# The second attention stage and the FP4 stage of a fused kernel in one block, with FP4's first steps and weight transposes inside attention's last steps

## Chip, cores, metric

One core of a Trainium2 chip. The metric is the device time of one execution in microseconds; the matrix engine is TensorE (PE), the others are VectorE (DVE), ScalarE (ACT), GpSimd (POOL) and SyncE (SP), which issues the transfers. All engines run their own instruction lists in order and meet at semaphores.

## What is computed

Two layers on `x` of 4 x 1024 rows with 256 columns. Each layer is cross attention to a context of 77 rows with 16 heads of 16, then a feed-forward part, each with a layer norm before it and a residual after it:

```
x = x + xattn0(layernorm(x), ctx)          # softmax(q k^T / 4) v, then Wo
x = x + ffn_sine(layernorm(x))             # W1 256x1024, a sine term, relu, W2
x = x + xattn1(ctx, layernorm(x), mask)    # the same with a mask per row and key
x = x + ffn_fp4(layernorm(x))

def ffn_fp4(x):                            # blocks of 16 along the last dim
    gate = q4(x) @ q4(w_gate).T            # 256 -> 704
    y    = q4(x) @ q4(w_up).T
    return q4(silu(gate) * y) @ q4(w_down).T
# q4: scale = max|block| / 6, values rounded to 0, .5, 1, 1.5, 2, 3, 4, 6 times scale
```

## The kernel before

The rows of `x` stay in the core's memory as 32 tiles of 128 rows (`T` = 32). Four stages follow one another: `attention(l=0)`, `ffn_sine`, `attention(l=1)`, `ffn_fp4`. Each is a `nc.Block()` with one unrolled list of instructions for each engine, and at a block's end all engines meet. Each stage is a software pipeline written out by hand: `step(i)` on an engine does its part of several tiles.

**Attention.** In `step(i)` PE does: the scores of tile i (into banks `psS0` to `psS3`), the transposes of the normalised tile i+1 (`psQ`), `attended(i-2)` (transposes of `on`, the attention output, into `psY`), then for tile i-1 the transposes of the shifted scores in three groups through one bank `psT`, each group waiting until ACT's exp (`prob`) has emptied the bank, with the queries of tile i+1 behind the first group and `projected(i-2)` (times Wo, into `psY`) behind the second, and last softmax times V of tile i-1 (`psO`). DVE does `outputs(i-2)` (reciprocal of the sums and division of `psO`, giving `on`), the row maxima and the shift of tile i, the low part of `oTs` for tile i-2 (`attended_high` on ACT is its high part), statistics of tile i+3, the low part of the queries, the normalised tile i+2, and `residual(i-2)`. Steps 5 to 27 that are odd also quantise one of 12 pieces of the FP4 weights `w4` (`w4_scales`, `w4_powers` on DVE, `w4_scale_up`, `w4_rounding` on POOL; the first attention stage does the other 12). `step(32)` and `step(33)` drain the pipeline: in step 32 (i == T) the calls of `attended(30)` and, on ACT, `attended_high(30)` come after the three groups and the three exps.

**FP4.** At the start of its block PE transposes the quantised weights in 11 `groups` through five banks: eight of three 128 x 128 transposes for `wgu` (gate and up; ACT writes the high part, `weight_copy`, and DVE the low part, `weight_low`), three of four for `wdT` (down; no low part). 36 transposes in all. PE waits for all of these before its `step(i)`. The steps run from -10 to 34. DVE: `bn_stats` and `bn_aggr` of tile i+10, the block maxima of tile i+4 (`x_largest`, `x_scale`, `x_inverse`), `x_powers` of tile i+3, `x_low` of tile i+2, `hidden`, `h_largest` and the rest of quantising `hid` for tiles i and i-1, `residual(i-2)`. POOL: `deviations` for four tiles at once, `x_up` (i+4), `x_sum`, `x_rounded`, `x_down` (i+3, giving `xres`), `h_up`, `h_down`. ACT: `normalise` (i+5), `x_lowered` (i+3), `x_high` (i+2), `h_kick` (i), the silu (i+1), the copies of transposed `hid`. PE: the products of tile i with gate and up in three segments of 512, 512 and 384 columns (`psGU`), of six matmuls each, the transposes of `xres` of tile i+1 behind the first segment, the down products of tile i-3, the transposes of `hres` of tile i-2. SP stores four tiles at a time.

Each tile's `hid` needs the silu of its gate half; the silu of tile 1 stands behind `h_kick(0)` on ACT, which needs `h_exponents(0)` on DVE, `h_up(0)` on POOL and `h_inverse(0)` on DVE, so PE's products of tile 2 wait for the whole chain from `hid` of tile 0.

Of the kernel before, what the change touches and what calls it, by code (L numbers as in the profile page):

```python
# [5 lines left out]
P = 128  # L6
# [66 lines left out]
def build(nc, x_in, ctx_in, mask_in, att0_in, att1_in, w1_in, w2_in, w4_in, cols_in, rows_in,  # L73
          blockmask_in, headmask_in, ident_in, out):
    with ExitStack() as ctx:
# [3 lines left out]
        def sem(name):  # L79
# [20 lines left out]
        w_high, w_split, w4_max, w4_scale, w4_inv, w4_scaled, w4_val, w4_exp, w4_pow, w4_sum, w4_round = (  # L100
            sem(n) for n in ("w_high", "w_split", "w4_max", "w4_scale", "w4_inv", "w4_scaled", "w4_val", "w4_exp",
                             "w4_pow", "w4_sum", "w4_round"))
# [9 lines left out]
        with ExitStack() as early:  # L112

            own(early, "w1", [P, 2, KC, FF0], F32R)
            own(early, "w2", [P, 2, FF0 // P, D], F32R)
            with ExitStack() as keys:
                own(keys, "kblk0", [P, 2, B, KC, PAIR * KV], F32R)
                own(keys, "wo0", [P, 2, KC, D], F32R)
                attention(nc, sem, 0, g)
            ffn_sine(nc, sem, g)  # L120
        with ExitStack() as keys:
            own(keys, "kblk1", [P, 2, B, KC, PAIR * KV], F32R)
            own(keys, "wo1", [P, 2, KC, D], F32R)
            attention(nc, sem, 1, g)
        own(ctx, "wgu", [P, 2, KC, 2 * FF1], F32R)
        own(ctx, "wdT", [P, NF1, D])
        ffn_fp4(nc, sem, g)


class Context:  # L130


    def __init__(self, nc, sem, g, l, ctx, psK, psVT, psV):
        self.nc, self.g, self.l, self.psK, self.psVT, self.psV = nc, g, l, psK, psVT, psV
        self.k_mm, self.k_high, self.k_low, self.vT_mm, self.vT_ready, self.v_mm, self.vblk_done = (
            sem(f"b{l}_{n}") for n in ("k_mm", "k_high", "k_low", "vT_mm", "vT_ready", "v_mm", "vblk_done"))
        self.bias_mm, self.bias_done, self.wo_high, self.first_keys, self.more_keys = (
            sem(f"b{l}_{n}") for n in ("bias_mm", "bias_done", "wo_high", "first_keys", "more_keys"))
        self.kTs = ctx.enter_context(nc.sbuf_tensor(f"b{l}_kTs", [P, 2, KC, B * KV], F32R))
        self.vT = ctx.enter_context(nc.sbuf_tensor(f"b{l}_vT", [P, KC, B, 3 * KV], F32))  # L140
# [23 lines left out]
    def value_transposes(self, pe):  # L164

        pe.wait_ge(self.vT_ready, KC)
        for n, (c, h, _, _) in enumerate(V_SLOTS):
            if n == 1:
                pe.wait_ge(self.bias_done, 1)
# [8 lines left out]
    def key_copies(self, act):  # L178
        bk = C_BK + 2 * self.l
        for h in range(KC):  # L180
            act.wait_ge(self.k_mm, h + 1)
# [3 lines left out]
    def value_copies(self, act):  # L185
        for h in range(KC):
            act.wait_ge(self.vT_mm, h + 1)
# [4 lines left out]
    def projection_high(self, act):  # L192
        self.nc.scalar.copy(self.g[f"wo{self.l}"][:, 0], self.g["wat"][self.l][:, :, 2 * D:3 * D]).then_inc(self.wo_high, 1)

    def head_block(self, b, n):

        return (self.g[f"kblk{self.l}"][:, :, b, :, n * KV:(n + 1) * KV],
# [1338 lines left out]
```

## Time and profile before

| | |
|---|---|
| Median of 3 runs | 1014.23 us (1012.83 to 1015.88) |
| The profiled execution | 1008.32 us, span 1006.5 us |
| Busy, share of the span | PE 92%, DVE 83%, ACT 48%, POOL 46% |
| Mean granted clock of PE | 0.966 of full |
| First attention stage | ends at 257.5 us |
| Sine stage | to about 476 us |
| Second attention stage | ends at 732.6 us |
| FP4 stage | from there to the end |

The times of the trace are microseconds from the start of the span. The span is what the engines' instructions cover; 1.8 us lie around it. PE's busy time holds its pipeline's latency, so that a PE that is busy all the time need not be at its peak. "Granted clock" is the share of TensorE's full 2.4 GHz that it was given; a value between 0.5 and 1 in a stretch means that it changed within the stretch.

### The profile page before, as it was taken

How to read it: one execution, taken by the hardware profiler on the slowest of the kernel's cores; microseconds unless marked ns; L12 is line 12 of the kernel's file. 1: busy time of each engine (PE TensorE's matmuls, PEld its weight loads, DVE VectorE, ACT ScalarE, POOL GpSimd, SP SyncE). 2: the span in 40 equal slices, each digit the busy share in tenths (PEclk: the TensorE clock that was granted, in tenths of full speed). 3: DMA queues.
4: the chain of work that ended last, by engine and by line, in shares of the span. 5: the costliest groups of instructions: out<-in, count | busy, mean ns of one | idle time of the engine just before them, and what ended most of it. 6: DMA issues, size and time to landing. Idle time of an engine off the chain costs nothing. (4 is left out here: it accounts for less than half of the span.)

```text
span 1006.5 us, 20339 instructions
## 1 busy us (share of the span) xinstructions
PE 927.3 (92%) x7332; PEld 817.8 (81%) x7332; DVE 832.3 (83%) x2172; ACT 486.8 (48%) x1019; POOL 466.7 (46%) x663
## 2 busy tenths in 40 slices
PE   6899999998599999998899999999868999999997
PEld 4798998997488888887689898989756888888885
DVE  5899999995599999986789888988468889889874
ACT  2643443442288888886344343433244444444442
POOL 2233333330376666664223323333046777777662
PEclk9999999998699999999899999999869999999999
DMA  9020000000000000000100000000000000000000
GB/s 349 19 96 2 2 2 2 1 2 1 1 1 2 1 1 1 1 1 4 49 2 2 2 2 2 2 1 2 1 1 1 22 22 1 21 22 22 22 21 22
DMA packets 6083, 18.32 MB, mean 18 GB/s; under 512 B 864, under 2 KB 2784, under 8 KB 5472
## 3 DMA queue, kind: packets, MB, share of 16 engines
q1 hardware_dynamic: 5264, 16.52, 4.3%
q8 instruction: 59, 0.97, 0.4%
q10 hardware_dynamic: 720, 0.50, 0.2%
q14 instruction: 40, 0.33, 0.1%
HBM read 12.83 MB, written 4.19 MB: 17 GB/s over the span
## 5 line engine op out<-in xcount | busy, mean ns | idle before, releaser
L815 PE MATMUL a_psO<-vblk,a_prob 128*128 128x51 f32 (+1 forms) x1280 | 151.9, 275 | 0.0
L815 PEld LDWEIGHTS a_psO<-vblk,a_prob 128*128 128x128 f32 x1280 | 151.6, 196 | 0.0
L1408 PE MATMUL f_psGU<-wgu,f_xTs 128*128 128x512 f32 (+1 forms) x576 | 141.7, 391 | 3.9 <-ACT f_silu L1360 2.6
L504 DVE TENSOR_REDUCE a_mx<-a_psS 128x4 f32<-128x308 f32 x256 | 115.0, 470 | 18.1 <-PE a_psS L737 16.5
L676 ACT COPY a_xTs<-a_psQ 128x256 f32<-128x256 f32 x64 | 23.9, 373 | 205.5 <-PE a_psQ L746 205.5
L687 ACT ACTIVATE a_prob<-a_psT 128x512 f32<-128x512 f32 (+1 forms) x192 | 101.1, 526 | 44.1 <-PE a_psT L793 42.7
L1408 PEld LDWEIGHTS f_psGU<-wgu,f_xTs 128*128 128x128 f32 x576 | 104.0, 193 | 19.6 <-DVE f_xTs L1172 4.6
L793 PE MATMUL a_psT<-ident,a_shifted 128*128 128x128 f32 x640 | 106.8, 282 | 12.4 <-ACT a_prob L687 9.5
L512 DVE TENSOR_TENSOR a_shifted<-a_psS,a_mx 128x308 f32<-128x308 f32 x256 | 114.4, 467 | 0.0
L1034 PEld LDWEIGHTS s_psY<-w,s_hid 128*128 128x128 f32 x768 | 99.4, 188 | 16.6 <-POOL s_hid L952 12.3
L1034 PE MATMUL s_psY<-w,s_hid 128*128 128x256 f32 x768 | 104.0, 284 | 5.7 <-POOL s_hid L952 5.0
L1022 PE MATMUL s_psH<-s_xTs,w 128*128 128x512 f32 x384 | 101.8, 402 | 2.7 <-DVE s_xTs L933 2.0
L952 POOL TENSOR_TENSOR s_hid<-wat,s_hid 128x512 fp32r<-128x512 f32 x64 | 86.1, 1346 | 39.1 <-ACT wat L989 39.1
L793 PEld LDWEIGHTS a_psT<-ident,a_shifted 128*128 128x128 f32 x640 | 72.7, 142 | 27.3 <-ACT a_prob L687 27.3
L1425 PE MATMUL f_psY<-wdT,f_hTs 128*128 128x256 f32 x384 | 89.8, 384 | 1.6 <-ACT f_hTs L1365 1.6
L1425 PEld LDWEIGHTS f_psY<-wdT,f_hTs 128*128 128x128 f32 x384 | 73.7, 193 | 13.4 <-issue 1.5
L1022 PEld LDWEIGHTS s_psH<-s_xTs,w 128*128 128x128 f32 x384 | 69.0, 191 | 15.5 <-DVE s_xTs L933 2.4
L644 POOL TENSOR_TENSOR a_rstd<-a_mv,expo 128x1 f32<-128x1 f32 x64 | 15.3, 239 | 141.3 <-DVE a_mv L580 141.2
L400 POOL TENSOR_TENSOR w4val<-w,w4scale 128x192 f32<-128x192 f32 x24 | 12.3, 513 | 140.7 <-DVE w4scale L393 140.7
L754 PE MATMUL a_psQ<-a_xTs,wat 128*128 128x128 f32 x512 | 72.5, 285 | 1.9 <-ACT a_xTs L676 1.8
L754 PEld LDWEIGHTS a_psQ<-a_xTs,wat 128*128 128x128 f32 x512 | 63.1, 194 | 5.5 <-ACT a_xTs L676 3.5
L763 PE MATMUL a_psY<-wo,a_oTs 128*128 128x256 f32 x384 | 63.3, 302 | 3.7 <-DVE a_oTs L541 3.7
(158 smaller groups left out, 1916.0 us busy)
## 6 DMA issues: line engine op xcount, KB each, us to landing
out_x<-x SPq DMA_DIRECT2D x8, 512.0 KB, 2.6
x<-in_x SPq DMA_DIRECT2D x3, 1024.0 KB, 12.1
w<-in_w SPq DMA_DIRECT2D x1, 2304.0 KB, 9.6
w<-in_w SPq DMA_DIRECT2D x2, 1024.0 KB, 16.9
a_mask<-in_mask SPq DMA_DIRECT2D x4, 308.0 KB, 4.0
wat<-in_att SPq DMA_DIRECT2D x1, 1024.0 KB, 20.7
x<-in_x SPq DMA_DIRECT2D x1, 768.0 KB, 8.3
wat<-in_att SPq DMA_DIRECT2D x2, 256.0 KB, 5.0
```

What stands on the lines that cost most here:

```text
L504: nc.vector.tensor_reduce(mx[:, u, j * BH:(j + 1) * BH], psS[j][:, 0:BH * KV].rearrange("p (h k) -> p h k", k=KV), AX.X, ALU.max).then_inc ...
L512: nc.vector.tensor_tensor(shifted[:, u, 0:HK].rearrange("p (c j n k) -> p j c n k", c=KC, j=NB, n=PAIR)[:, j], psS[j][:, 0:BH * KV].rearra ...
L687: nc.scalar.activation(prob[:, v, c0 * P:c1 * P], psT[:, 0:(c1 - c0) * P], ACT.Exp, scale=scale).then_inc(prob_ready, 1)
L754: mm = nc.tensor.matmul(psQ[:, h * P:(h + 1) * P], wat[:, k, h * P:(h + 1) * P], xTs[:, u, k * P:(k + 1) * P], start=(k == 0), stop=(k == ...
L763: mm = nc.tensor.matmul(psY[:, 0:D], oTs[:, u, a, k * P:(k + 1) * P], wo[:, b, k, :], start=(m == 0), stop=(m == len(terms) - 1))
L793: mm = nc.tensor.transpose(psT[:, (c - c0) * P:(c - c0 + 1) * P], shifted[:, v, c * P:(c + 1) * P], ident[:])
L815: mm = nc.tensor.matmul(psO[:, CH[c] * VW:(CH[c] + n) * VW], prob[:, v, c * P:(c + 1) * P], vblk[:, t // R, c * NJ * VW:(c * NJ + n) * VW] ...
L952: nc.gpsimd.tensor_tensor(hid[:, f % 4, 1, :], full[:, f % 2, :], hid[:, f % 4, 0, :].bitcast(F32), ALU.subtract).then_inc(hid_low, 1)
L1022: mm = nc.tensor.matmul(psH[f2 % 4][:], w1[:, a, k, f2 * P:(f2 + 1) * P], xTs[:, u if f + AHEAD < NF else 1 - u, b, k, :], start=(m == 0), ...
L1034: mm = nc.tensor.matmul(psY[q // 2][:, q % 2, :], hid[:, f0 % 4, a, q * P:(q + 1) * P], w2[:, b, f0, :], start=(f0 == 0 and q % 2 == 0 and ...
L1408: mm = nc.tensor.matmul(psGU[:, n0:n1], xTs[:, u, a, k * P:(k + 1) * P], wgu[:, b, k, n0:n1], start=(n == 0), stop=(n == len(TERMS) - 1))
L1425: mm = nc.tensor.matmul(psY[:, 0:D], hTs[:, 1 - u, c * P:(c + 1) * P], wdT[:, c, :], start=(c == 0), stop=(c == NF1 - 1))
```

## The change

- `ffn_fp4` becomes a class `Fp4` whose methods give each engine's steps; `attention` takes it as `tail`. For l = 1, attention and FP4 are one block; the engines no longer meet between the two.
- FP4's step j runs after attention's step j + 34 on DVE, POOL and ACT for j = -10 to -2 (attention steps 24 to 32), so with the statistics from step 24 on, `normalise` from step 29, the block maxima from step 30. Step -1 is on DVE inside attention's step 33, behind `outputs(31)`, and on ACT and POOL behind that step. PE's step -1 (the transposes of `xres` of tile 0) comes at the end of attention's step 32, and its step 0 (products of tile 0, transposes of tile 1) in step 33 between `attended(31)` and `projected(31)`.
- The weight transposes stand in attention's step 32 on PE: groups 0 and 1 behind the first `psT` group, 2 and 3 behind the second, 4 to 7 behind `projected(30)`, 8 to 10 behind softmax times V of tile 31. They use four banks, those of `psS`, instead of five. The copies on ACT and DVE are put beside them. PE waits for POOL's last w4 piece by a new semaphore, `w4_done`.
- In both attention stages `attended(30)` and `attended_high(30)` in step 32 move from behind the third group and exp to behind the second.
- FP4's large buffers (`silu`, `hid`, `hval`, `hpow`, `hres`, `hTs`) and its banks are laid over attention's, whose buffers are reordered so that the ones still in use are left alone; attention's transposed V (`vT`) is laid over `prob`. Semaphores of the keys are shared by the two attention stages and count on.

```diff
-def attention(nc, sem, l, g):
+def attention(nc, sem, l, g, tail=None):
...
+        vT = prob[:].rearrange("p u n -> p (u n)")[:, 0:KC * B * 3 * KV].rearrange("p (h b n) -> p h b n", h=KC, b=B)
...
+        if tail:
+            ctx.close()
+            tail.open(ctx)
...
             @block.vector
...
                     if valid(i - 2):
                         outputs(i - 2, u)
+                    if tail and i == T:
+                        tail_pads()
+                        for n in range(2):
+                            weight_low(n)
+                    if tail and i == T + 1:
+                        tail_step(-1)
...
                     if valid(i - 2):
                         residual(i - 2)
+                    if tail and i == T:
+                        for n in range(2, tail.LOWS):
+                            weight_low(n)
...
+                    if tail and tail.FIRST <= i - T - 2 < -1:
+                        tail_step(i - T - 2)
+                if tail:
+                    for i in range(0, tail.LAST):
+                        tail_step(i)
...
             @block.scalar
...
-                    if i == T:
-                        attended_high(i - 2, u)
+                        if tail and i == T and n == 0:
+                            for m in range(2):
+                                weight_copy(m)
+                        if i == T and n == 1:
+                            attended_high(i - 2, u)
+                            if tail:
+                                for m in range(2, 4):
+                                    weight_copy(m)
...
                     if 0 < i < B:
                         context.later_keys(act, i)
+                    if tail and i == T:
+                        for n in range(4, tail.LOWS):
+                            weight_copy(n)
+                    if tail and tail.FIRST <= i - T - 2:
+                        tail_step(i - T - 2)
+                    if tail and i == T:
+                        for n in range(tail.LOWS, len(tail.groups)):
+                            weight_copy(n)
...
             @block.tensor
...
                             if n == 1 and valid(i - 2) and i != T:
                                 projected(i - 2, u)
+                            if tail and i == T and n < 2:
+                                weight_transposes(2 * n, 2 * n + 2)
+                            if i == T and n == 1:
+                                attended(i - 2, u)
                     else:
                         queries(i + 1, v)
-                    if i == T:
-                        attended(i - 2, u)
+                    if tail and i == T + 1:
+                        tail_step(0)
                     if valid(i - 2) and i >= T:
                         projected(i - 2, u)
+                    if tail and i == T:
+                        weight_transposes(4, tail.LOWS)
...
+                    if tail and i == T:
+                        weight_transposes(tail.LOWS, len(tail.groups))
+                        tail_step(-1)
+                if tail:
+                    for i in range(1, tail.LAST):
+                        tail_step(i)
...
+        self.psGU = ps("psGU", [P, 3 * 512])
+        self.psM = ps("psM", [P, 2 * 512])
...
+        self.banks = [self.psGU[:, 0:512], self.psGU[:, 512:1024], self.psGU[:, 1024:1536], self.psM[:, 0:512]]
...
+        def weight_transposes(n0, n1):
+            if n0 == 0:
+                pe.wait_ge(self.g["w4_done"], W4_PIECES)
+            for n in range(n0, n1):
+                parts = groups[n][0]
+                wait(pe, w_copied, n - 3)
+                wait(pe, w_low, min(n - 3, LOWS))
+                for q, src in enumerate(parts):
+                    mm = nc.tensor.transpose(banks[n % 4][:, q * P:(q + 1) * P], src, ident[:])
+                mm.then_inc(w_mm, 1)
```

## Rows read from the trace of the kernel before

**Rows 1.** Busy time by stretch: from:to, length, each engine's busy us, PE clock, DMA.
```profile
510.00:700.00 190.00, 188.59 (x2027) 170.70 (x2027) 166.89 (x538) 73.37 (x188) 64.77 (x129) 1.00 0.01 2
...
715.00:730.00 15.00, 11.11 (x72) 9.68 (x72) 4.88 (x14) 3.44 (x8) 0.00 (x0) 0.82 0.00 0
730.00:745.00 15.00, 8.76 (x42) 7.84 (x42) 11.16 (x41) 7.28 (x16) 2.93 (x5) 0.61 0.01 2
```
**Rows 2.** Timeline of PE, the seam: start, length, engine, line, operation, count, [idle before].
```profile
719.07 0.64 PE L793 MATMUL a_psT<-ident,a_shifted 128*128 128x128 f32 x4
...
724.18 3.89 PE L815 MATMUL a_psO<-vblk,a_prob 128*128 128x51 f32 x20
...
732.92 2.15 PE L1460 MATMUL f_psGU<-ident,w 128*128 128x128 f32 x9 [0.78 <-PEq L488]
...
746.22 0.66 PE L1433 MATMUL f_psB<-ident,f_xres 128*128 128x128 f32 x2 [5.10 <-POOL f_xres L1282]
748.11 2.93 PE L1408 MATMUL f_psGU<-wgu,f_xTs 128*128 128x512 f32 x6 [1.24 <-DVE f_xTs L1172]
...
761.07 1.98 PE L1408 MATMUL f_psGU<-wgu,f_xTs 128*128 128x512 f32 x6 [2.62 <-ACT f_silu L1360]
...
773.05 2.69 PE L1408 MATMUL f_psGU<-wgu,f_xTs 128*128 128x512 f32 x12
```
**Rows 3.** Timeline of DVE, the start of the FP4 stage.
```profile
733.25 0.43 DVE L1242 BATCH_NORM_STATS2 f_st<-x 128x6 f32<-128x256 f32 x1
733.71 0.18 DVE L1249 BATCH_NORM_AGGREGATE f_mv<-f_st 128x2 f32<-128x6 f32 x1
...
737.28 0.46 DVE L1219 TENSOR_TENSOR wgu<-f_psM,wgu 128x320 fp32r<-128x320 f32 x1
...
747.63 0.42 DVE L1172 TENSOR_TENSOR f_xTs<-f_psB,f_xTs 128x256 fp32r<-128x256 f32 x1
...
748.55 0.41 DVE L1158 TENSOR_REDUCE f_xam<-f_xhat 128x16 f32<-128x256 f32 x1
...
754.29 0.89 DVE L1193 TENSOR_TENSOR f_hid<-f_silu,f_psGU 128x704 f32<-128x704 f32 x1 [1.70 <-PE f_psGU L1408]
```
**Rows 4.** Timeline of PE, attention's step 26.
```profile
678.21 0.38 PE L746 MATMUL a_psY<-ident,a_on 128*128 128x128 f32 x2
678.43 0.60 PE L793 MATMUL a_psT<-ident,a_shifted 128*128 128x128 f32 x4
```
**Rows 5.** Timeline of ACT, the start of the FP4 stage.
```profile
735.75 0.43 ACT L1373 CAST wgu<-f_psM 128x320 fp32r<-128x320 f32 x1 [0.16 <-PE f_psM L1460]
...
740.23 0.59 ACT L1373 COPY wdT<-f_psM 128x512 f32<-128x512 f32 x1 [0.17 <-PE f_psM L1460]
...
751.95 1.28 ACT L1360 ACT_TABLE_LOAD   x1
```
**Rows 6.** Timeline of DVE, the ends of attention's steps 24 and 25.
```profile
669.51 0.26 DVE L495 RECIPROCAL a_rden<-a_psO 128x16 f32<-128x16 f32 x1 [0.60 <-PE a_psO L815]
...
677.17 0.26 DVE L411 TENSOR_SCALAR w4pow<-w4pow 128x192 f32<-128x192 f32 x1
...
677.63 0.42 DVE L498 TENSOR_TENSOR a_on<-a_psO,a_rden 128x256 f32<-128x256 f32 x1
```
**Rows 7.** Timeline of POOL, FP4's tile 0.
```profile
742.42 0.62 POOL L1267 TENSOR_TENSOR f_xval<-f_xhat,f_xinv 128x256 f32<-128x256 f32 x1 [3.67 <-ACT f_xinv L1336]
```
**Rows 8.** Busy time and PE clock in short stretches.
```profile
763.00:764.00 1.00, 1.00 (x5) 0.90 (x4) 0.96 (x4) 0.30 (x2) 0.00 (x0) 0.50 0.00 0
...
243.00:244.00 1.00, 0.64 (x3) 0.64 (x4) 0.00 (x0) 0.31 (x1) 0.00 (x0) 0.68 0.00 0
```
**Rows 9.** Timeline of PE, step 32 of the first attention stage.
```profile
243.36 1.12 PE L793 MATMUL a_psT<-ident,a_shifted 128*128 128x128 f32 x4 [0.69 <-ACT a_prob L687]
...
247.20 1.65 PE L763 MATMUL a_psY<-wo,a_oTs 128*128 128x256 f32 x6 [0.92 <-DVE a_oTs L541]
```
**Rows 10.** The tile `shifted`: engine, operation, count: ns min/median/max, first and last start.
```profile
L512 DVE TENSOR_TENSOR a_shifted<-a_psS,a_mx x256: 465/467/473, 18.6 to 716.9; 128x308 f32<-128x308 f32 x128
```

More of the change, by code:

```diff
@@ L659, in _ @@
                     inputs.fill(pool)
+                if tail:
+                    tail_step = tail.gpsimd(pool)
                 for i in range(FIRST, LAST):
                     step(i, i % 2)
+                    if tail and tail.FIRST <= i - T - 2:
+                        tail_step(i - T - 2)
+                if tail:
+                    for i in range(0, tail.LAST):
+                        tail_step(i)
             @block.scalar
@@ L709, in _ @@
                 context.value_copies(act)
+                if tail:
+                    tail_step, weight_copy = tail.scalar(act)
                 for i in range(0, LAST):
@@ L715, in _ @@
                         context.later_keys(act, i)
+                    if tail and i == T:
+                        for n in range(4, tail.LOWS):
+                            weight_copy(n)
+                    if tail and tail.FIRST <= i - T - 2:
+                        tail_step(i - T - 2)
+                    if tail and i == T:
+                        for n in range(tail.LOWS, len(tail.groups)):
+                            weight_copy(n)
+                if tail:
+                    for i in range(0, tail.LAST):
+                        tail_step(i)
             @block.tensor
@@ L832, in _ @@
                     step(i, i % 2)
+                if tail:
+                    tail_step, weight_transposes = tail.tensor(pe)
                 for i in range(0, LAST):
@@ L1047, in _ @@
                 run_steps(step, FIRST, LAST, LOOP_FROM)
[L1050 to L1060 removed]
+NX, NH = D // QB, FF1 // QB
+OUT_TILES = 4
+SG = 4
+KICK = 1.5 * 2.0 ** 22
+SEGMENTS = ((0, 512), (512, 1024), (1024, 2 * FF1))
@@ L1478, with stores @@
+    def stores(self, sp):
+        x, out, x_done, stored = self.g["x"], self.g["out"], self.x_done, self.stored
+        for t in range(0, T, OUT_TILES):
+            b, r = t // R, t % R
+            sp.wait_ge(x_done, t + OUT_TILES)
+            sp.dma_start(out[b].rearrange("(p r) d -> p r d", r=R)[:, r:r + OUT_TILES, :],
+                         x[:, t:t + OUT_TILES, :]).then_inc(stored, 16)
+        sp.wait_ge(stored, 16 * (T // OUT_TILES))
 def kernel(x, ctx_1024, mask_BxSxS2_ik0, L0_xattn_Wq, L0_xattn_bq, L0_xattn_Wk, L0_xattn_bk, L0_xattn_Wv, L0_xattn_bv,
```

813 lines of the change are left out of this document (415 added, 398 removed).

## Prediction

> **What bounds the kernel now.** Start with the windows by stretch [rows 1]. In the second attention stage (510 to 700 us) TensorE (PE) is busy for 188.6 of 190 us: that stage goes at PE's pace, and VectorE (DVE), busy for 166.9, has 23 us to spare. From 715 to 745 us PE is busy for only 19.9 of 30 us, and the granted clock falls to 0.82 and 0.61 of full: this is the seam between the last attention steps and the FP4 stage. The timeline of PE shows the seam piece by piece [rows 2]. Attention's step 32 begins with the transposes at 719.07. Softmax times V of the last tile (at 724.18) runs at half clock. The 36 weight transposes begin at 732.92; then nothing comes until the transposes of FP4's tile 0 at 746.22, and its first products start at 748.11. DVE's timeline [rows 3] gives the mark that I count to: the first `hid` at 754.29. From `hid` of tile 0 on, each tile needs the chain over DVE, ACT and POOL that holds the third tile's products until 761.07 [rows 2], and the same code runs before and after. So the question is how much earlier `hid` of tile 0 starts, and what the kernel pays for it. Below, time 0 is 719.07, and `hid` of tile 0 is at 35.22.
>
> **Prices.** At full clock one 128-column transpose issues each 0.11 us (two at 678.21, the next group at 678.43 [rows 4]); at half clock about 0.22 (nine in 2.15, row 732.92 [rows 2]). A weight group of three costs PE 0.33, one of four 0.43. A weight copy on ACT is 0.43 (a little more for the wider groups), that of the last three 0.59 [rows 5]; a `weight_low` on DVE is 0.46 [rows 3]. Successive operations overlap by some 0.09, and a hand-over costs 0.05.
>
> **Part 1: statistics in attention steps 24 to 29.** `bn_stats` and `bn_aggr` of one tile take 0.46 + 0.13 = 0.6 us of DVE (starts 733.25 and 733.71 and the second one's 0.18 [rows 3]) after each of these steps. After an even step DVE has an idle 0.60 before the next output (the one at 669.51 [rows 6]), which takes them. After steps 25 and 27, which also quantise a piece of w4, it has none: its last power at 677.17 is followed at once by the reciprocal and the division at 677.63, which ends 678.05 [rows 6], and PE takes that result at 678.21 [rows 4]. There the 0.6 less the slack of 0.16 is a stall of 0.45 on PE, twice: **+0.9**. Nothing would make it less than 0; if all eight steps from 24 to 31 stalled in full it would be +4.8. I take 0.9 since the slack of each kind of step is in the rows. ACT and POOL are not on the path here.
>
> **Part 2: step 32, with eight weight groups in it.** PE: first psT group 0 to 0.43, weight groups 0 and 1 to 1.08, second psT group at 1.33 (it waits for ACT's exp), groups 2 and 3 to 2.40, `attended(30)` to 2.62, third psT group to 2.90. ACT: exp 0.68 to 1.28, two weight copies to 2.02, second exp to 2.63, the high part of `attended(30)` to 3.20, two copies, third exp to 4.23. The copies delay that high part by little, because it now comes before the third exp. DVE's low part ends at 3.67, the projection issues 3.72 to 4.55, groups 4 and 5 follow to 5.20. Groups 6 and 7 wait for their bank, that is for `weight_low` 2 and 3, which stand behind `residual(30)` on DVE: they end at 6.38. Softmax times V then takes 2.17 to 8.55. Before it began at 5.11, so the eight groups push it back by 1.3; but 24 of the 36 transposes are now done.
>
> **Part 3: the wait that is added.** DVE's `tail_step(-2)` holds `x_low(0)`, and `outputs(31)` is queued behind it; so is everything that needs tile 31's attention output: `attended(31)`, which PE has placed ahead of FP4's first products. `x_low(0)` needs PE's transposes of tile 0, which come after weight groups 8 to 10: 8.55 + 1.30 + 0.22, done 10.25; ACT's copy of them ends 10.65. POOL has tile 0 ready long before: `x_up` waited for `xinv` until 742.42 [rows 7], and this chain now starts in step 31, with statistics done six steps earlier. DVE from `x_low` to the next tile operation took 747.63 to 748.55 = 0.92 [rows 3]: 11.62. `outputs(31)` 0.7, so `attended(31)` at 12.4 and FP4's first products at 12.65. The last three weight copies stand behind ACT's copy of tile 0 and end at 12.2, just hidden: another 0.5 there would be paid in full. PE has nothing from 10.07 to 12.4, a pause of 2.3 us.
>
> **Part 4: FP4's tile 0.** Its 18 products and two transposes at full clock take 1.48 + 0.14 + 2.69 = 4.31 (the 2.69 is row 773.05 [rows 2]): 16.95. The table load of 1.28 [rows 5] stands behind ACT's copy of tile 1, as before, and the silu ends at 16.9. But the projection of attention's tile 31 is now behind these products on PE (issue to 17.6, done 17.8), and `residual(31)` is ahead of `hid(0)` on DVE: `hid` at **18.2**, 1.2 later than the products allow. The barrier with its 0.8 us between the stages is gone and is within these figures.
>
> Gain so far: 35.22 - 18.2 - 0.9 = **16.1 us at full clock.**
>
> **Part 5: the clock.** The rows show falls from 2.4 GHz to 1.2 GHz after PE had been idle: it had nothing to do for the 2.62 us before 761.07 [rows 2], and at 763 it had half the clock [rows 8]. My schedule has a pause of 2.3 us of the same kind, so I charge one such fall on tile 0's products: row 748.11 has 2.93 for six at half clock, where half of the 2.69 plus the last one's drain is 1.5, and transposes and other products add a little: **+1.5**. The bounds are 0 (no fall) and 6.9 (half clock from 4.5 on: groups 4 to 7 +0.8, softmax times V +1.8 from row 724.18, groups 8 to 10 and both small transposes +1.8, tile 0's products +1.8, the last projection +0.7). The Trainium skill says (TensorE: Matmul & The Clock Gate, section "Part 1: The HAM clock gate") that throttled is the default state and recent activity releases it; by that rule the pause brings a fall, as the trace has it, and the denser step 32 should keep what came before it at full clock, which is the one-fall case, 16.1 - 1.5. No run here shows the denser step yet.
>
> **Part 6: attention's first stage.** It gets the new place of `attended` too. In the kernel before, the third psT group waited for exp, and the transposes of `on`, ACT's copy and DVE's low part came after it, so that the projection began at 247.20, 0.92 us late [rows 9]. Now these transposes follow the second group, and their copy comes before the third exp: ACT at 245.2 instead of 246.32, and with it the rest: **1.1 us earlier**. Bounds 0 and 1.3.
>
> **Nothing** is charged for the new addresses of the buffers, the shared semaphores, and V's transposed copy laid over `prob`: before the change the two attention stages have their buffers at different places and `shifted` is written in 465 to 473 ns in all 256 cases [rows 10]; V's copy is read on PE before the first exp in PE's own order. The transposes of the pieces of w4 wait for POOL's last piece, from step 27, five steps earlier. The stores move to the queue of the mask loads, which are long done. FP4's later steps keep their order and their time.
>
> **Sum:** 16.1 - 1.5 + 1.1 = 15.7 us. The profiled execution took 1008.32 with a span of 1006.5, so 992.6 for its like. The median of the runs shown is 1014.23, 5.9 above it, within nothing that the change touches; I predict 1014.23 - 15.7 = **998.5 us**.
>
> **Rivals.**
> A. Half clock through the whole seam: 16.1 - 6.9 + 1.1 = 10.3, so 1003.9. For it: the first stage's clock was down to 0.68 in the stretch at 243, after spells of only 0.69 without work in the same step [rows 8, 9]. Against: 3.9 us of transposes fill them now. 22%.
> B. DVE cannot take the added work: all eight steps stall, +4.8 instead of 0.9: gain 11.8, 1002.4. For it: DVE has nothing to spare after odd steps with a w4 piece; against: it has 0.60 after the even ones [rows 6], and steps 29 and 31 have no piece. 10%.
> C. No fall and no stall in part 1: gain 18.1, 996.1. 10%.
> D. No net gain: the pause behind `x_low(0)` grows. If the copies of part 2 and tile 0's copy queued so that `attended(31)` came at 28 instead of 12.4, nothing would be left: 1014. Nothing in the rows is that long. 2%.
> E. Slower: attention's DVE operations become longer at the new addresses. In the steps with a w4 piece DVE is within 0.16 of PE's pace (part 1), so a longer DVE step shows; +0.3 in each of 64 steps costs 19, less 15.7: 1017.7. It decides from 0.25 a step on. The even durations speak against it [rows 10]. 4%.
> My forecast: 52%.
>
> **Numbers.** Range 995.5 to 1005.0: each case has a spread of some 2 us about its time (the schedule is worked, and the runs of one kernel lie 3 us apart); the range holds my forecast nearly whole, B, two thirds of A and of C, which makes 8 in 10. A difference of 0.3% (3 us) is what the measurement can tell from no change; faster by more 0.94, within it 0.02, slower by more 0.04.
>
> **What would show it.** Weight transposes between the psT groups; `attended(31)` of the second stage about 12 to 13 us after step 32's first transposes, first products right behind, `hid` of tile 0 near 18 to 20 us; 0.45 us of waiting for `on` on PE in steps 26 and 28 and none in 25, 27 and 29; the projection of the first stage 1.1 us earlier; FP4's pace from tile 4 on as before. I am wrong if half clock lasts from the eighth weight group on (A), if all steps from 24 on take over 7.5 us (B), or if FP4's later tiles have new idle spells.

## The result, and the profile after

The changed kernel takes 988.6 us (median of 4 runs, 987.04 to 994.16) where the kernel before takes 1014.62 (median of 4, 1012.83 to 1015.88): 26.0 us less, a ratio of 0.976 [0.974, 0.979]. I had predicted 998.5 us with a range of 995.5 to 1005.0, so the sign was right and the size was wrong by 9.9 us: the time lies below the whole range. The profiled execution took 987.04 (span 985.2), 21.3 less than the profiled one before.

First the windows of the changed kernel by stretch (from:to, length, busy us of PE, PEld, DVE, ACT, POOL, then PE's granted clock, the DMA engines' share and GB/s).

```profile
25.00:50.00 25.00, 22.04 (x196) 20.55 (x194) 18.44 (x48) 12.39 (x24) 4.97 (x6) 0.80 0.07 28
235.00:255.00 20.00, 16.08 (x145) 14.09 (x143) 10.01 (x28) 5.79 (x14) 0.00 (x0) 1.00 0.00 1
...
470.00:495.00 25.00, 19.11 (x164) 15.98 (x164) 14.82 (x46) 5.18 (x11) 6.33 (x12) 1.00 0.17 52
510.00:700.00 190.00, 188.05 (x2013) 170.14 (x2010) 169.19 (x546) 74.23 (x190) 64.11 (x128) 1.00 0.01 2
...
715.00:730.00 15.00, 12.10 (x100) 10.95 (x99) 10.46 (x36) 8.87 (x23) 6.54 (x10) 1.00 0.01 2
730.00:745.00 15.00, 11.91 (x61) 9.96 (x61) 10.37 (x28) 6.61 (x15) 8.02 (x11) 1.00 0.00 1
```

Two things are to be seen. The seam, 0.82 and 0.61 of full clock before [rows 1], is at full clock throughout, although PE isn't busy for 6 of these 30 us. And the clock differs in stretches outside the seam, most of which I had not looked at as terms of the sum: 235 to 255 and 470 to 495 are at full clock now, and 25 to 50 has less than before. The kernel before has this there:

```profile
25.00:50.00 25.00, 21.09 (x211) 19.12 (x209) 21.26 (x55) 14.99 (x30) 5.71 (x7) 0.93 0.06 21
235.00:255.00 20.00, 15.67 (x111) 13.51 (x110) 6.82 (x19) 4.27 (x9) 0.00 (x0) 0.71 0.00 1
...
470.00:495.00 25.00, 20.36 (x134) 17.03 (x134) 12.81 (x39) 6.78 (x14) 7.67 (x13) 0.86 0.16 52
```

Not all of this is the change's doing. In a second trace of the kernel before (`c_before`, experiment 1) 470 to 495 is at 1.00. It is the first stage's drain, the work from its step 32 to its end, that differs between the old and the new order in every trace (experiments 2 and 3).

The timeline of PE in the changed kernel's seam, which answers to [rows 2] (in brackets: idle before, and what ended it):

```profile
716.84 0.63 PE L840 MATMUL a_psT<-ident,a_shifted 128*128 128x128 f32 x4
717.30 0.82 PE L1572 MATMUL f_psGU<-ident,w 128*128 128x128 f32 x6
...
723.42 2.32 PE L868 MATMUL a_psO<-vblk,a_prob 128*128 128x51 f32 x20
725.57 1.51 PE L1572 MATMUL f_psGU<-ident,w 128*128 128x128 f32 x12
726.91 0.38 PE L1541 MATMUL f_psB<-ident,f_xres 128*128 128x128 f32 x2
729.09 0.44 PE L793 MATMUL a_psY<-ident,a_on 128*128 128x128 f32 x2 [1.79 <-DVE a_on L501]
729.28 1.63 PE L1513 MATMUL f_psGU<-wgu,f_xTs 128*128 128x512 f32 x6
...
741.43 1.63 PE L1513 MATMUL f_psGU<-wgu,f_xTs 128*128 128x512 f32 x6 [3.09 <-ACT f_silu L1463]
```

And DVE's timeline there, which answers to the end of [rows 3]:

```profile
727.74 0.42 DVE L1258 TENSOR_TENSOR f_xTs<-f_psB,f_xTs 128x256 fp32r<-128x256 f32 x1 [1.64 <-ACT f_xTs L1450]
...
728.61 0.42 DVE L501 TENSOR_TENSOR a_on<-a_psO,a_rden 128x256 f32<-128x256 f32 x1
...
734.33 0.42 DVE L525 TENSOR_TENSOR x<-x,a_psY 128x256 f32<-128x256 f32 x1 [1.66 <-PE a_psY L810]
734.67 0.88 DVE L1279 TENSOR_TENSOR f_hid<-f_silu,f_psGU 128x704 f32<-128x704 f32 x1
```

Counted from step 32's first transposes (716.84), `attended(31)` comes at 12.25, the first products at 12.44, `hid` of tile 0 at 17.83. The wait that the change lengthens is the row with 1.79 (0.81 before): PE stands until DVE's `on`, which is queued behind `x_low(0)`. `residual(31)` at 734.33 is what starts `hid` last.

### The profile page after: what moved, and what is told of

Read it like the earlier page. It is cut to its first block and busy times, and to the rows that moved or that the text cites. A ratio compares the mean times of both kernels' runs of the same rounds, so it can differ in the third digit from the quotient of the medians.

```text
span 985.2 us, 20329 instructions
## 1 busy us (share of the span) xinstructions
PE 912.7 (93%) x7332; PEld 806.9 (82%) x7332; DVE 830.7 (84%) x2172; ACT 485.3 (49%) x1019; POOL 465.8 (47%) x663
## 5 line engine op out<-in xcount | busy, mean ns | idle before, releaser
L868 PEld LDWEIGHTS a_psO<-vblk,a_prob 128*128 128x128 f32 x1280 | 149.6, 194 | 0.0
L1513 PE MATMUL f_psGU<-wgu,f_xTs 128*128 128x512 f32 (+1 forms) x576 | 138.5, 385 | 3.1 <-ACT f_silu L1463 3.1
L507 DVE TENSOR_REDUCE a_mx<-a_psS 128x4 f32<-128x308 f32 x256 | 115.1, 470 | 17.4 <-PE a_psS L784 15.8
L1513 PEld LDWEIGHTS f_psGU<-wgu,f_xTs 128*128 128x128 f32 x576 | 101.9, 189 | 17.7 <-DVE f_xTs L1258 3.4
L1095 PEld LDWEIGHTS s_psY<-w,s_hid 128*128 128x128 f32 x768 | 99.4, 188 | 16.6 <-POOL s_hid L1013 12.2
L987 DVE TENSOR_SCALAR s_turn<-s_arg 128x512 f32<-128x512 f32 x64 | 51.7, 808 | 14.7 <-ACT s_arg L1063 13.5
```

The lines of the kernel that those rows point to most:

```text
L507: nc.vector.tensor_reduce(mx[:, u, j * BH:(j + 1) * BH], psS[j][:, 0:BH * KV].rearrange("p (h k) -> p h k", k=KV), AX.X, ALU.max).then_inc ...
L868: mm = nc.tensor.matmul(psO[:, CH[c] * VW:(CH[c] + n) * VW], prob[:, v, c * P:(c + 1) * P], vblk[:, t // R, c * NJ * VW:(c * NJ + n) * VW] ...
L987: nc.vector.tensor_scalar(k, a, MAGIC, MAGIC, ALU.add, ALU.subtract).then_inc(turn_set, 1)
L1095: mm = nc.tensor.matmul(psY[q // 2][:, q % 2, :], hid[:, f0 % 4, a, q * P:(q + 1) * P], w2[:, b, f0, :], start=(f0 == 0 and q % 2 == 0 and ...
L1513: mm = nc.tensor.matmul(psGU[:, n0:n1], xTs[:, u, a, k * P:(k + 1) * P], wgu[:, b, k, n0:n1], start=(n == 0), stop=(n == len(TERMS) - 1))
```

## The experiments

**How the time at half clock is read.** Each run comes with its span and its mean granted clock; the clock has only the levels 1.2 and 2.4 GHz, so a run was at half clock for 2 x (1 - mean) x span. The table has the mean of this over the runs of a kernel. "Ratio" is to the kernel before in the same session.

| kernel | median us (runs) | ratio [95%] | us at half clock |
|---|---|---|---|
| before, all sessions | 1012.8 to 1014.6 | 1 | 74 |
| `c_before` | 1015.2 (12) | 1.001 [0.999, 1.004] | 77 |
| `e_move` | 1006.2 (7) | 0.994 [0.991, 0.997] | 55 |
| `e_serial` | 1008.9 (12) | 0.995 [0.993, 0.998] | 64 |
| `e_wt` | 1003.6 (5) | 0.989 [0.987, 0.991] | 54 |
| `e_lead` | 997.9 (6) | 0.985 [0.982, 0.988] | 50 |
| `e_nomove` | 994.0 (6) | 0.982 [0.979, 0.986] | 50 |
| changed | 988.6 (4) | 0.976 [0.974, 0.979] | 39 |
| `a_again` | 989.5 (6) | 0.977 [0.974, 0.981] | 38 |
| `a_sched` | 989.1 (4) | 0.976 [0.974, 0.978] | 37 |
| `a_fill` | 990.5 (6) | 0.977 [0.974, 0.979] | 32 |
| `a_best` | 988.7 (6) | 0.975 [0.973, 0.978] | 30 |
| `e_fillseam` | 1008.4 (12) | 0.996 [0.994, 0.998] | 51 |
| `e_fill` | 1002.3 (6) | 0.990 [0.987, 0.993] | 25 |

**1. The kernel before again**, nothing edited: do its own runs differ by the clock?

> The kernel before once more, to see the granted clock of each of its runs beside its time. Theory C (clock): the extra gain of some 10 us beyond my sum is time at half clock that the change removes, and it differs from run to run. Then the runs near 1014 us have a lower mean clock than the profiled one of 1008.3 us (0.966): 0.945 to 0.96, and time and clock go together, as in the changed kernel (987.0 at 0.986, 994.2 at 0.972, which is 0.25 us for each us at half clock). Theory S (structure): the extra gain is in the structure (addresses, the engines' meeting, a chain that I sized wrongly), and the clock of the runs at 1014 is 0.966 like that of 1008.3.

They do in part. Over these 12 runs time and time at half clock go together (correlation 0.81). But the runs near 1014 us have a clock of 0.960 to 0.966, not 0.945 to 0.96 as expected, and two profiled executions of this one kernel have the same clock and spans 7.0 us apart, so the clock isn't all of it. The cores' view, before and `c_before`:

```profile
core 0: 1006.5 us, clock 0.966
```
```profile
core 0: 1013.5 us, clock 0.966
```

**2. The new place of `attended(30)` alone**, in the kernel before, both attention stages; first the lines of ACT, then those of PE.

```diff
-                    if i == T:
-                        attended_high(i - 2, u)
+                        if i == T and n == 1:
+                            attended_high(i - 2, u)
...
+                            if i == T and n == 1:
+                                attended(i - 2, u)
...
-                    if i == T:
-                        attended(i - 2, u)
```

> The kernel before with part 6 alone: attended(30) and its copy behind the second group in step 32 of both attention stages. By my sum 1.1 us in the first stage and 0.9 in the second: 2 us faster. Theory C: the drain of the first stage stays at full clock more often (softmax times V 2.3 instead of 4.3), so 4 to 7 us faster and a mean clock higher by 0.005 to 0.01. Theory S: 2 us and the same clock.

7.0 us faster, for an edit that takes 0.9 us of waiting out of each of two steps. PE's timeline of the first stage in `e_move`:

```profile
244.62 0.64 PE L793 MATMUL a_psT<-ident,a_shifted 128*128 128x128 f32 x4
245.94 0.66 PE L793 MATMUL a_psT<-ident,a_shifted 128*128 128x128 f32 x4 [0.69 <-ACT a_prob L687]
246.43 0.38 PE L746 MATMUL a_psY<-ident,a_on 128*128 128x128 f32 x2
247.28 0.44 PE L793 MATMUL a_psT<-ident,a_shifted 128*128 128x128 f32 x2 [0.47 <-ACT a_prob L687]
248.01 0.97 PE L763 MATMUL a_psY<-wo,a_oTs 128*128 128x256 f32 x6 [0.28 <-DVE a_oTs L541]
248.82 2.31 PE L815 MATMUL a_psO<-vblk,a_prob 128*128 128x51 f32 x20
...
260.32 1.97 PE L1044 MATMUL s_psX<-ident,wat 128*128 128x128 f32 x8 [6.05 <-DVE wat L900]
```

The same stretch of the kernel before, beside [rows 9]:

```profile
242.04 0.64 PE L793 MATMUL a_psT<-ident,a_shifted 128*128 128x128 f32 x4
...
248.65 4.31 PE L815 MATMUL a_psO<-vblk,a_prob 128*128 128x51 f32 x20
...
263.10 1.97 PE L1044 MATMUL s_psX<-ident,wat 128*128 128x128 f32 x8 [6.06 <-DVE wat L900]
```

From the first group to the sine stage it is 15.7 us instead of 21.1. The order itself gives about 0.9 of this: in `c_before`, where the clock is still full up to the projection, the projection begins 4.31 us after step 32's first transposes,

```profile
249.86 1.42 PE L763 MATMUL a_psY<-wo,a_oTs 128*128 128x256 f32 x6 [0.98 <-DVE a_oTs L541]
```

and in `e_move` 3.39 us after them. The rest is that softmax times V takes 2.31 where it took 4.31, and the matmuls beside it likewise. The four traces with the old order and no fillers here take 19.4 to 21.1 us for this stretch, the nine with the new order 15.7 to 16.4. In the seam the trace of `e_move` shows no gain (35.9 us from step 32 to `hid` of tile 0, where the two traces of the kernel before have 35.2 and 36.8), so the gain that the traces show lies in the first stage's drain.

**3. The changed kernel with the old place in the first stage alone.**

```diff
-                        if i == T and n == 1:
+                        if tail and i == T and n == 1:
                             attended_high(i - 2, u)
...
+                    if not tail and i == T:
+                        attended_high(i - 2, u)
```
(and the same for `attended` on PE)

> The changed kernel with the old order of attended in the first attention stage only. By my sum 1.1 us slower than the changed kernel (990 us). Theory C: 4 to 6 us slower (993 to 995), with the spell at half clock from the first stage's step 32 on in the profile, as in the kernel before. Theory S: 990.

5.4 us slower than the changed kernel (4.5 against its second measurement, `a_again`), and its first stage has the old rows again:

```profile
251.50 1.65 PE L811 MATMUL a_psY<-a_wo,a_oTs 128*128 128x256 f32 x6 [0.92 <-DVE a_oTs L550]
252.95 4.31 PE L871 MATMUL a_psO<-vblk,a_prob 128*128 128x51 f32 x20
```

**4. One block, new addresses, moved `attended`, but nothing of FP4 inside attention**: lead and weight transposes behind its last step, as in the kernel before. The lines of DVE and PE (ACT and POOL likewise):

```diff
-                    if tail and tail.FIRST <= i - T - 2 < -1:
-                        tail_step(i - T - 2)
...
+                    for i in range(tail.FIRST, tail.LAST):
...
+                    weight_transposes(0, len(tail.groups))
+                    for i in range(-1, tail.LAST):
```

> One block with the new addresses and the moved attended, but nothing of FP4 inside attention: lead and weight transposes come after it in their old order (with four banks). Theory C: the barrier's 0.8 us and what e_move gains, so 3 to 8 us faster than before (1007 to 1011), with the seam at half clock as before. Theory S (addresses or the meeting of the engines carry the extra gain): 12 or more faster (below 1003).

1008.9: 2.7 above `e_move`, with 8 us more at half clock. What is placed inside attention is thus worth 19 to 20 us of the 26. One block, the new addresses and the shared semaphores make nothing faster by themselves, since `e_serial`, which has them, isn't faster than `e_move`.

**5. and 6. One half of the placement each.** `e_lead` keeps FP4's lead steps inside attention (step -1 on PE alone) and puts all weight transposes behind the last projection; `e_wt` keeps the transposes and puts the lead behind.

```diff
-                            if tail and i == T and n < 2:
-                                weight_transposes(2 * n, 2 * n + 2)
...
+                    weight_transposes(0, len(tail.groups))
```
```diff
-                        tail_step(-1)
...
+                    for i in range(-1, tail.LAST):
```

> The changed kernel with FP4's lead inside attention as changed, but all 11 weight groups behind attention's last projection, ahead of FP4's tile 0. By full-clock prices the transposes and their copies (eleven on ACT, some 0.48 each) put 5 us on the path where attended(31) and the projection are done earlier: hid of tile 0 some 3 us later than in the changed kernel. Theory C adds the drain without transposes, which falls to half clock as in the kernel before: 4 to 7 slower than the changed kernel, 993 to 996 in all. Theory S: 3 slower and the same clock.

> The changed kernel with the weight transposes inside attention's step 32 as changed, but FP4's steps -10 to -1 behind attention on all engines. The lead's chain over DVE, POOL and ACT took from 733.25 to 748.11 before, of which DVE spent 3.5 on weight_low: 11 us on the path with PE idle. By full-clock prices 10 us slower than the changed kernel; theory C adds a spell at half clock behind it: 11 to 14 slower, 1000 to 1003. Theory S: 10.

Both are slower than expected: `e_lead` with 997.9 us by 2 us beyond its range, `e_wt` with 1003.6 by 0.6. Against `e_serial`, the lead alone gives 11.0 us, the transposes alone 5.3, and both together 20.3 (`e_serial` to the changed kernel). By the medians that is 4.0 more than the two apart, by the ratios about 2, which the intervals don't tell from nothing. The traces say it better. From step 32's first transposes to `hid` of tile 0 they have 33.8 us in `e_serial`, 25.5 in `e_lead`, 30.6 in `e_wt` and 17.8 in the changed kernel: 8.3 and 3.2 for the halves, 15.9 for both. With both halves inside, tile 0's products on PE could move inside as well. `e_lead` was expected to have `hid` of tile 0 3 us later than the changed kernel, and it is 7.7 later, with a spell at half clock from 725 to 740.

**7. and 8. PE kept at work in the kernel before.** Transposes of the identity into an unused bank, of no use to anyone, fill the waits of the drains of both attention stages, of the sine stage's start and of FP4's lead (`e_fill`), or only those between the second attention stage and FP4 (`e_fillseam`, without the sine stage's lines and with `l and` in the condition of attention's).

```diff
+                def fill(n, bank):
+                    for _ in range(n):
+                        nc.tensor.transpose(bank, ident[:], ident[:])
...
+                            if i == T and n < 2:
+                                fill(4, psQ[:, 0:P])
...
+                            if s == -1: 
+                                fill(44, psY[0][:, 0, 0:P])
...
+                fill(40)
```

> The kernel before with idle PE filled: transposes of the identity into banks that nobody reads, ahead of the waits in the drains of both attention stages (4 to 6 each), at the sine stage's start (44 and 14) and in FP4's lead (40, 8 and 18), fewer than fit into each wait at full clock. No other instruction is moved. Theory C: time at half clock falls from 74 us to under 35 us on the mean, and at 0.25 to 0.33 us for each the kernel becomes 9 to 13 us faster (1000 to 1004) though PE has more work. Theory S: no gain, or slower by what the transposes delay (up to 3).

> The kernel before with the filling transposes of e_fill only in the second attention stage's drain and in FP4's lead. It tells how much of e_fill's 10.5 us lies in the seam. Theory C: the seam holds 24 to 27 us at half clock in both profiles of the kernel before, the first stage's drain and the sine stage's start 24 to 27 as well; so about half, 4 to 6 us faster (1007 to 1009).

Work for nothing makes the kernel 10.5 us faster by the median, though no instruction of use has moved and PE has more to do. Windows of `e_fill`; the kernel before has 0.71 from 235 to 255 and 0.82 from 715 to 730:

```profile
247.00:258.00 11.00, 9.68 (x79) 8.49 (x79) 2.63 (x7) 2.21 (x5) 0.00 (x0) 1.00 0.01 1
258.00:266.00 8.00, 6.94 (x62) 6.53 (x61) 4.49 (x13) 0.51 (x2) 5.65 (x12) 1.00 0.01 3
...
716.00:735.00 19.00, 15.81 (x126) 13.67 (x125) 9.05 (x28) 6.29 (x15) 0.00 (x0) 1.00 0.00 0
```

The execution that was profiled is the slowest of `e_fill`'s six, 1009.4 us, 1.1 more than the profiled one before. The table of stretches at the end of this section shows why: it is faster where the fillers stand, by 8.3 us in all, and slower in places that the edit doesn't touch, 5.7 us of it before the first stage's step 32.

Of the 10.5, the seam's fill gives 4.5 (`e_fillseam`). That leaves 6 for the first stage's end and the sine stage's start, which were not filled by themselves.

**9. The waits that are left in the changed kernel.** Four edits: statistics of FP4's tiles 0 to 4 behind attention's even steps 20 to 28; `outputs(31)` ahead of `x_low(0)`; PE's wait for the last three weight copies moved to the products that read them; `residual(31)` behind `hid(0)`.

```diff
-                    if valid(i - 2):
+                    if tail and i == T + 1:
+                        tail_step(-2, lambda: outputs(i - 2, u))
+                    elif valid(i - 2):
                         outputs(i - 2, u)
...
+                        for j in {20: (-10,), 22: (-9,), 24: (-8,), 26: (-7,), 28: (-6,)}.get(
+                                i, (i - T - 2,) if 28 < i < T else ()):
+                            tail_step(j)
...
+                    tail_step(0, None, lambda: residual(T - 1))
```

> The changed kernel with four edits of the order: the statistics of FP4's tiles 0 to 4 behind even attention steps only (20 to 28), outputs(31) ahead of x_low(0), PE's wait for the last three weight copies put off to where each is needed, residual(31) behind hid(0) on DVE. By the trace of the changed kernel: the two stalls of 0.4 on PE in steps 26 and 28 gone, PE's pause before attended(31) (1.79) shorter by 1.1, hid of tile 0 another 0.9 earlier: 2.5 to 3 faster than the changed kernel, 986.

The order came out as meant: `hid` of tile 0 starts at 732.50, 16.5 after step 32's first transposes instead of 17.8, and the waits in steps 26 and 28 are gone. The time did not move. PE's timeline in `a_sched`:

```profile
739.61 1.63 PE L1524 MATMUL f_psGU<-wgu,f_xTs 128*128 128x512 f32 x6 [2.70 <-ACT f_silu L1472]
741.08 0.59 PE L1553 MATMUL f_psB<-ident,f_xres 128*128 128x128 f32 x2
741.32 4.15 PE L1524 MATMUL f_psGU<-wgu,f_xTs 128*128 128x512 f32 x12
```

Twelve products take 4.15 instead of 2.69: the clock fell here, behind a wait of 2.70, and in the profile of the changed kernel it did not behind one of 3.09 at the same place. But this fall isn't what ate the gain, as I thought when I wrote down what to expect of `a_best`. `a_best` has the same order and no fall here, and takes as long from `hid` of tile 0 to that of tile 31 (232.8 us; `a_sched` 232.9, the changed kernel 232.5). What `a_sched` gained up to `hid` of tile 0 (0.9 in steps 24 to 31, 1.35 in the seam) it gave back elsewhere, most of it, 1.7, in FP4's drain, where the down products of one of the last tiles ran at half clock (2.83 in the changed kernel):

```profile
973.10 4.52 PE L1545 MATMUL f_psY<-wdT,f_hTs 128*128 128x256 f32 x12 [0.55 <-ACT f_hTs L1477]
```

**10. The changed kernel again**, beside the next two.

> The changed kernel again, unchanged, on the chip of the three beside it: 987 to 991 on the median, and time again goes with time at half clock (0.25 to 0.33 us for each us). It is what a_fill and a_best are compared with.

989.5. This execution of the same code does fall at that place (`a_again`; the changed kernel's row at 741.43 has 1.63 for these six):

```profile
740.58 2.90 PE L1513 MATMUL f_psGU<-wgu,f_xTs 128*128 128x512 f32 x6 [3.07 <-ACT f_silu L1463]
...
747.75 0.63 PE L1555 MATMUL f_psA<-ident,f_hres 128*128 128x128 f32 x4 [0.26 <-POOL f_hres L1388]
```

And it costs nothing. Some 2.6 us of PE's time are lost to the half clock here, but PE then waits 0.26 us for `hres`, where it waited 2.88 us in the changed kernel's profile (748.61), and from `hid` of tile 0 to that of tile 31 both executions take 232.5 us. In these tiles the chain over DVE, ACT and POOL sets the pace.

**11. and 12. The changed kernel with fillers in the first stage's drain and the sine stage's start** (`a_fill`), and this with the four edits of `a_sched` (`a_best`).

```diff
+                            if not tail and i == T and n == 0:
+                                fill(4, psQ[:, 0:P])
...
+                            if s == -1:
+                                fill(44, psY[0][:, 0, 0:P])
```

> The changed kernel with transposes of the identity in the idle time of PE in the first attention stage's drain (4 and 2, 5 and 6) and at the sine stage's start (44 and 14). In the changed kernel's profile half clock lasts from 255 to 270 us (13.7 us). Theory C: this spell goes, mean time at half clock 25 us instead of 39, and 2 to 4 us are gained (985 to 987). Theory S: nothing is gained (989).

> a_fill and a_sched together. a_sched alone brought hid of tile 0 forward by 2.2 us in its profile, but a spell at half clock at 741 took 1.5 of it, and the median did not move. Theory C: with the filled first stage 983 to 986, the best of all. If edits of the order are worth nothing beside the clock: that of a_fill.

Both miss: 990.5 and 988.7 can't be told from the changed kernel. The windows of `a_fill`:

```profile
240.00:262.00 22.00, 18.96 (x156) 16.94 (x155) 10.55 (x30) 4.42 (x10) 5.41 (x12) 1.00 0.01 2
470.00:495.00 25.00, 20.51 (x125) 16.45 (x124) 14.25 (x45) 5.18 (x11) 5.23 (x11) 0.80 0.15 51
```

The half clock at the first stage's end is gone, and 470 to 495, at full clock in the changed kernel, is at 0.80, as it is in `a_best`. By the table below, `a_fill` gains 1.4 us in the sine stage and loses 3.2 in the second stage. Over all runs the time at half clock went down by only 7 to 9 us, which is 2 to 3 us of time by the fit below. The fillers themselves cost nothing at the first stage's end: from step 32 to the sine stage `a_fill` takes the same 15.7 us as the changed kernel.

**The stretches of seven traces**, in us, each from one mark to the next: step 32's first transposes of the first stage, the sine stage's first transposes, the second stage's first scores, its step 32's first transposes, `hid` of tile 0, `hid` of tile 31, the end of the span.

| trace | to step 32 | to sine stage | to second stage | to its step 32 | to `hid` 0 | to `hid` 31 | to the end |
|---|---|---|---|---|---|---|---|
| before | 242.0 | 21.1 | 213.7 | 242.2 | 35.2 | 232.6 | 19.6 |
| `c_before` | 245.6 | 20.0 | 214.1 | 244.0 | 36.8 | 233.7 | 19.3 |
| `e_fill` | 247.8 | 16.6 | 212.5 | 243.9 | 32.6 | 234.9 | 19.4 |
| changed | 245.4 | 15.7 | 214.0 | 241.8 | 17.8 | 232.5 | 18.1 |
| `a_again` | 244.7 | 15.7 | 213.9 | 241.7 | 17.8 | 232.5 | 18.1 |
| `a_sched` | 244.3 | 16.4 | 214.5 | 240.9 | 16.5 | 232.9 | 19.7 |
| `a_fill` | 244.9 | 15.7 | 212.5 | 244.9 | 17.8 | 232.5 | 19.3 |

## Why the prediction was wrong

**The schedule was right.** Each figure is from step 32's first transposes: `attended(31)` forecast at 12.4, measured 12.25; first products 12.65 and 12.44; `hid` of tile 0 18.2 and 17.83. The pause that part 3 derived, from `x_low(0)` ahead of `outputs(31)`, is there (1.8 us; I had 2.3). Part 1 is right in its place: `attended` waits in steps 26 and 28 alone. The waits on record are 0.27 and 0.25 where I had 0.45 each, and the steps from 24 to 31 together lose 0.8 where I had 0.9 (changed kernel, PE):

```profile
675.60 0.44 PE L793 MATMUL a_psY<-ident,a_on 128*128 128x128 f32 x2 [0.27 <-DVE a_on L501]
...
690.33 0.44 PE L793 MATMUL a_psY<-ident,a_on 128*128 128x128 f32 x2 [0.25 <-DVE a_on L501]
```

FP4 takes 232.5 us from `hid(0)` to `hid(31)`, before 232.6. Nothing for the addresses was right: `shifted` takes 465 to 471 ns at the new ones,

```profile
L515 DVE TENSOR_TENSOR a_shifted<-a_psS,a_mx x256: 465/469/471, 19.2 to 714.6; 128x308 f32<-128x308 f32 x128
```

and `e_serial` differs from `e_move` by no more than its clock explains. Rivals B, D and E fall with these, and A with the seam's full clock. C, no fall and no stall, had the right clock in the seam, but at 996.1 it misses too: the rest wasn't in the seam.

**The step that failed is the clock, in parts 5 and 6.** Between the two profiled executions the 21.3 us are:

| stretch | predicted | measured |
|---|---|---|
| start to first stage's step 32 | 0 | -3.4 |
| first stage's step 32 to sine stage (part 6) | +1.1 | +5.3 |
| sine stage and second stage's start | 0 | +1.1 |
| attention steps 24 to 31 (part 1) | -0.9 | -0.8 |
| seam at full clock (parts 2 to 4) | +17.0 | +17.4 |
| one fall on tile 0 (part 5) | -1.5 | 0 |
| FP4's steps | 0 | +0.2 |
| FP4's drain | 0 | +1.5 |
| sum | +15.7 | +21.3 |

*Part 6* is the term most mis-sized: forecast 1.1 us, measured 5.3. It priced the order at full clock, and as that it was near (0.9, experiment 2), though [rows 8] and the 1.65 for six matmuls in [rows 9] stood there to say that the clock was down. Experiments 2 and 3 give the term from both sides: 5.4 us as the last step of the change, and 7.0 for both stages on the old kernel. I had used these rows for rival A, a clock that gets worse, and never for the gain from a clock that gets better.

*Part 5* charged a fall on tile 0's products behind the pause before `attended(31)`. It didn't come in any of the four traces that have this pause with its 1.79 us (the changed kernel, `a_again`, `a_fill`, `e_nomove`): the first six products take 1.63 in each. So 1.5 was charged for nothing. Where the clock does fall, in three of these four, is two tiles later, behind the wait of 3.07 for the silu, and there it costs nothing (experiment 10).

*By chance.* The -3.4, the +1.1 and the +1.5 of the table aren't the change's. No trace has a shorter first stretch than the profiled execution before, and `e_move`, `e_fillseam` and `c_before`, in which nothing ahead of its end is edited, need 2.3 to 3.5 us more for it. The +1.5 is a spell at half clock in FP4's drain (994 to 998 in the kernel before). All eight traces with such a spell, `a_sched` and `a_fill` among them, have 19.3 to 19.8 us there, the six without it 18.1, and `e_move`, whose FP4 stage is the old one, is one of the six. The +1.1 goes with a spell from 485 to 493 in the kernel before, near which other traces, of either kernel, have one or none.

*The median.* The last 4.7 us are that the profiled execution before lay 6.3 under its median and the profiled one after 1.6 under its own. I called such a distance "within nothing that the change touches", and that was partly wrong. Some of it is time at half clock, in stretches all over the kernel, and the change touches that: 74 us before, 39 after. Within single kernels, all 14 pooled, a microsecond more at half clock goes with 0.32 us more of time. But the profiled execution before, at 68 us of half clock, had only 6 us less of it than the mean, which is 2 us of time. The rest of its distance is not explained, and it may be luck. With these 4.7 us and the 5.6 by which the table's sums differ the miss is complete: 26.0 us for a forecast of 15.7.

How much of the gain is clock can only be estimated. By the slope of 0.32 the 35 us less at half clock are worth 11 us, and both kernels without any half clock would take 989.8 and 977.2, 12.6 apart. The slope is a correlation, and slower runs could have more half clock because they wait more. The fillers are an intervention, and give less: 10.5 us for 49 us of half clock, 0.21 for each, by which the 35 us are worth 7.5. So of the 24 us between the means of all runs (1013.3 to 989.7) a third to a half is clock, by these estimates, and the rest order. The seam's 17.4 is itself partly clock: much of the 35.22 us it had before was at half speed, and `e_fillseam`, which moves nothing ahead, gets 4.5 us there (its trace has 32.6 for the same stretch).

*The range.* It gave each case 2 us, with three runs 3 us apart behind it. In the 24 runs of one session the kernel before lies between 1008.3 and 1019.0.

Seventy-four of 1011 us are at half clock in the kernel before, and 74 x 0.32 = 24 us is 2.3% of it. The Trainium skill (TensorE: Matmul & The Clock Gate, section "Part 1: The HAM clock gate") advises to model the ramp at under 1% of a typical kernel's span. That is said of the warm-up of a kernel, and the clock here falls again and again: the profile before has seven spells at half clock between 35 and 998 us, so the advice can't be taken for their sum.

The Trainium skill's same page (section "HAM oscillation — how this bites in real kernels") counts half of the throttled time as lost. This case has less: 0.32 by the slope and 0.21 by the fillers, since part of the slow work lies beside waits that are there anyway, as on FP4's tile 2 in `a_again`. By the page's half, the 35 us would be 17, an estimate.

**Open.** What decides in a given execution whether a pause brings a fall was not settled: the same code falls or doesn't at 740. Nor was it for the early spells and those at 470 to 495 in `a_fill` and `a_best`, and the 5.7 us by which traces differ before the first step 32 aren't all clock: `e_fill` and `e_fillseam` have the same time at half clock there (13.6 us) and are 3.4 us apart. No experiment here controls these. That the four edits of `a_sched` gain nothing in the median has no test of its own: its trace has them gain 1.8 us net, and lose it to the clock in stretches that they don't touch. `a_best` doesn't show a gain either. No version beat the changed kernel by what can be measured.

## What to carry to other kernels

Before summing a change on a PE-bound kernel, list every stretch where the granted clock is below full in the profile before, in all stages, and price the change against each of them: an edit that takes a microsecond of waiting out of a drain gave 5. Then ask whether PE sets the pace there: where it waits for another engine anyway, a fall can cost nothing. Take the expected time from the median with its mean clock, not from the one profiled execution, and give a fall that "should" happen a chance instead of a certainty. A cheap test of what the clock is worth is to fill the waits with useless matmuls: what the time falls by is clock, and needs no new order of the work. Here that was 10 us, and the new order gave 26 with its share of the clock.

## What the runs showed of the hardware

- A pause doesn't fix the clock's course. In the changed kernel pauses of 1.79 and 3.09 us, each behind dense work, left it at full; with the same code 3.07 brought half clock in another execution. In the first stage before, three pauses of 0.69 to 0.92 between short groups stood in a stretch at 0.71. In the second stage of the same execution such pauses (0.69, 0.69 and 0.98) left the groups at full-clock lengths until softmax times V.
- What a spell at half clock costs depends on what waits for PE. In the first stage's drain it took softmax times V from 2.31 to 4.31 us and the stretch from 15.7 to 19.4 or more; in FP4's drain it cost 1.2 to 1.7 us (18.1 against 19.3 to 19.8); on FP4's tile 2 it cost 0.0 (232.5 both ways).
- Runs of one unchanged kernel spread over 11 us (1008.3 to 1019.0 in 24 runs), and the time at half clock goes with it (correlation 0.82).
- Extra matmuls can shorten a kernel: `e_fill` issues some 170 more transposes and is 1.0% faster.
